# Decays, the copy of B and the order of products in a Mamba scan loop on one Trainium2 core

## What the kernel computes

```python
def step(h, inp):
    xh_t, B_t, C_t, dt_t, dA_t = inp
    h = dA_t[..., None, None] * h + (dt_t[..., None] * xh_t)[..., None] * B_t[:, None, None, :]
    y = jnp.einsum('bhpn,bn->bhp', h, C_t)
    return (h, y)
...
y = y + D[None, None, :, None] * xh
y = y * jax.nn.silu(z)
```

## Time and profile before

| what | value |
|---|---|
| median of 3 runs | 1082.24 us (1082.21 to 1082.91) |
| the profiled execution | 1084.32 us |
| its span in the profile | 1082.6 us |
| passes of the scan loop, DVE's first `dtx` to its last `H` | 741.62 to 825.32 us of the span, 83.7 us |
| busy in those 83.7 us | PE 64.6, DVE 63.7, POOL 48.3, ACT 24.0 us |

### The profile page before, as it was taken

How to read it: one execution, slowest core, us unless ns; L and a number is a source line. 1 busy time by engine, 2 the same in 40 slices (tenths; PEclk the granted TensorE clock), 3 DMA queues, 4 the chain that set the end, 5 groups by cost and what they waited for, 6 DMA issues and landing times. The chain is left out here.

```text
span 1082.6 us, 21285 instructions
## 1 busy us (share of the span) xinstructions
PE 949.9 (88%) x7613; PEld 563.9 (52%) x7613; DVE 801.6 (74%) x2128; ACT 681.7 (63%) x1049; POOL 500.9 (46%) x542
## 2 busy tenths in 40 slices
PE   3899999999999999969999999645878249999998
PEld 1323333333333333328878888323657238878886
DVE  7789999999989999755776554696675675775553
ACT  5226666666666665556888888583233138888886
POOL 4401201110121011116989999226562028989997
PEclk9869999999999999889999999887788669999999
DMA  4940322142222500025765675000000045667873
GB/s 104 248 154 17 102 78 58 40 132 51 58 80 84 100 3 3 2 68 154 192 186 148 196 194 133 20 1 0 0 0 1 3 104 161 198 171 168 213 193 97
DMA packets 80614, 105.93 MB, mean 98 GB/s; under 512 B 18252, under 2 KB 41602, under 8 KB 80514
## 3 DMA queue, kind: packets, MB, share of 16 engines
q1 hardware_dynamic: 78631, 102.43, 35.9%
q10 hardware_dynamic: 1883, 2.21, 0.7%
HBM read 95.84 MB, written 8.52 MB: 96 GB/s over the span
## 5 line engine op out<-in xcount | busy, mean ns | idle before, releaser
L801 POOL TENSOR_TENSOR f_act_low<-f_act,f_act_high 128x512 fp32r<-128x512 f32 x272 | 348.3, 1298 | 140.6 <-ACT f_act_high L777 132.8
L1710 DVE CUSTOM_DVE_ANT_0 at_rows<-at_rows,at_table_max 128x512 f32<-128x512 f32 x512 | 342.7, 717 | 38.6 <-PE at_rows L1488 29.0
L1657 ACT ACTIVATE at_prob<-at_cols 128x1024 f32<-128x1024 f32 x256 | 248.2, 1021 | 160.2 <-PE at_cols L1529 160.2
L816 DVE SCALAR_TENSOR_TENSOR f_gated<-f_hid,f_cw 128x512 f32<-128x512 f32 x256 | 176.0, 691 | 131.3 <-ACT f_act L782 91.4
L782 ACT ACTIVATE f_act<-f_gated 128x512 f32<-128x512 f32 x272 | 171.8, 632 | 85.7 <-DVE f_gated L816 68.1
L777 ACT CAST f_act_high<-f_act 128x512 fp32r<-128x512 f32 x272 | 164.7, 606 | 0.0
L1529 PE MATMUL at_cols<-at_table_cols,flip_sum 64*64 64x512 f16 x2048 | 138.4, 383 | 0.0
L1541 PE MATMUL at_pv<-at_prob,at_v_stack 128*32 128x512 f32 x1024 | 138.1, 612 | 0.4 <-ACT at_prob L1657 0.4
L1488 PE MATMUL at_rows<-at_k_stack,at_q_stack 48*64 48x512 bf16 x1024 | 117.0, 403 | 4.4 <-DVE at_maxima L1710 3.7
L748 PE MATMUL f_acc<-f_act_high,wd_high 128*128 128x512 f32 x272 | 107.8, 396 | 3.8 <-POOL f_act_low L801 3.8
L748 PE MATMUL f_acc<-f_act_low,wd_high 128*128 128x512 f32 x272 | 106.2, 391 | 0.0
(11 more groups left out here) (341 smaller groups left out, 1281.1 us busy)
## 6 DMA issues: line engine op xcount, KB each, us to landing
f_cw<-f_c_rows SPq DMA_DIRECT2D x256, 256.0 KB, 4.4
at_table_cols<-bias_rows SPq DMA_DIRECT2D x64, 124.0 KB, 4.3
at_table_max<-bias_rows SPq DMA_DIRECT2D x12, 480.0 KB, 4.6
at_q_stack<-q_parts SPq DMA_DIRECT2D x32, 96.0 KB, 2.5
at_k_stack<-k_parts SPq DMA_DIRECT2D x24, 96.0 KB, 3.4
at_raw_weights<-in_L_ffn_up_w_dram SPq DMA_DIRECT2D x8, 256.0 KB, 4.0
at_raw_weights<-in_L_ffn_down_w_dram SPq DMA_DIRECT2D x8, 256.0 KB, 5.1
at_table_max<-bias_rows ACTq DMA_DIRECT2D x4, 480.0 KB, 5.7
```

The lines of the kernel that those rows point to most:

```text
L801: nc.gpsimd.tensor_tensor(act_l[:, n % PART_SLOTS, :], act[:, n % ACT_SLOTS, :], act_h[:, n % PART_SLOTS, :].bitcast(F32), ALU.subtract).t ...
L816: ins = nc.vector.scalar_tensor_tensor(out=gated[:, n % GATE_SLOTS, :], in0=hid[:, n % HID_SLOTS, :], scalar=0.0, in1=cw[:, k % C_SLOTS, u ...
L1657: act(prob[:, S % 2, 2 * hp:2 * hp + 2, :], s2[:, hp, :, :], ACT.Exp).then_inc(exp_done, 1)
L1710: nc.vector.tensor_tensor_reduce(out=slot, in0=slot, in1=t_max[:, 2 * p.hp + j, c:c + BANK][:, ::-1], scale=1.0, scalar=-3.0e38, op0=ALU.a ...
```

## The change

`M` takes the decays from their PSUM bank, where ACT's exponential now leaves them; `E` is gone. The copy of B goes from DVE to ACT, behind the exponential of the same b and behind a wait on `dtx`. On DVE, `Ht` moves behind the `M` of its b, and both `dx` behind both `M`. On PE, both `inter` stand ahead of everything else that follows, and `dh` waits for `dx` as well, since `dx` reads the bank that the next pass's transposes overwrite.

```diff
-        E = sb("E", [P, 2, SH, P])
...
                         mm(ps[:, pb + 2, P:P + INNER], xch[:, b, 3, :], H[:, b, :, :].rearrange("p h c -> p (h c)"),
                            start=True, stop=True).then_inc(inter_done, 1)
-
+                    for b in range(SEQS):
+                        pb = 4 * b
                         pe.wait_ge(M_ready, n + (b + 1))
...
                         pe.wait_ge(btok_ready, n + (b + 1))
+                        pe.wait_ge(dx_ready, n + (b + 1))
...
-                        act(E[:, b, :, :], ps[:, 4 * b, :], ACT.Exp).then_inc(E_ready, 1)
+                        act(ps[:, 4 * b, :], ps[:, 4 * b, :], ACT.Exp).then_inc(E_ready, 1)
+                        a.wait_ge(dtx_ready, n + (b + 1))
+                        nc.scalar.copy(btok[:, b, :], ps[:, 4 * b + 1, INNER:INNER + P]).then_inc(btok_ready, 1)
...
-                        nc.vector.tensor_copy(btok[:, b, :], ps[:, pb + 1, INNER:INNER + P]).then_inc(btok_ready, 1)
-                        v.wait_ge(y3_ready, n + (b + 1))
-                        tt(dx[:, b, :, :], tok, dsk[:].unsqueeze(2).broadcast_to([P, SH, HEAD_COLS]), ALU.mult).then_inc(dx_ready, 1)
                         v.wait_ge(gt_done, n + (b + 1))
                         tt(Gm[:, b, :], ps[:, pb + 2, 0:P], m.upto[:], ALU.mult).then_inc(gm_ready, 1)
+                    for b in range(SEQS):
+                        t = bass.ds(i + b * SEQ_CHUNKS, 1)
+                        v.wait_ge(E_ready, n + (b + 1))
+                        v.wait_ge(gm_ready, n + (b + 1))
+                        tt(M[:, b, :, :], ps[:, 4 * b, :].rearrange("p (h j) -> p h j", h=SH), Gm[:, b, :].unsqueeze(1).broadcast_to([P, SH, P]),
+                           ALU.mult).then_inc(M_ready, 1)
                         tt(Ht[:, b, :, :], H[:, b, :, :],
...
                     for b in range(SEQS):
-                        v.wait_ge(E_ready, n + (b + 1))
-                        v.wait_ge(gm_ready, n + (b + 1))
-                        tt(M[:, b, :, :], E[:, b, :, :], Gm[:, b, :].unsqueeze(1).broadcast_to([P, SH, P]),
-                           ALU.mult).then_inc(M_ready, 1)
+                        tok = ps[:, 4 * b + 1, 0:INNER].rearrange("p (h c) -> p h c", h=SH)
+                        v.wait_ge(y3_ready, n + (b + 1))
+                        v.wait_ge(btok_ready, n + (b + 1))
+                        tt(dx[:, b, :, :], tok, dsk[:].unsqueeze(2).broadcast_to([P, SH, HEAD_COLS]), ALU.mult).then_inc(dx_ready, 1)
```

## The result

| | before | after |
|---|---|---|
| median | 1083.03 us (6 runs, 1082.21 to 1085.4) | 1073.89 us (6 runs, 1070.41 to 1076.57) |
| profiled execution, its span | 1084.32, 1082.6 us | 1073.45, 1071.7 us |
| scan loop, first `dtx` to last `H` | 83.70 us | 67.70 us |

The ratio is 0.9924 (95% interval 0.9907 to 0.9942), a gain of 9.1 us. The sign was right; 1073.89 lies far outside 1054 to 1064.5.

The account below looks back on a forecast made before the run. DVE and PE were taken to wait on each other in turn, with `M` held by POOL's `R`. The loop falls from 83.42 to 58.52 us, taking 1084.3 to 1059.4; less 2.1 to the median, 1057.3, range 1054 to 1064.5.

Parts of the forecast that it names:

- the price: `M` on DVE in the scan, one input now in PSUM: no longer held, 0.84 us less in each of seven passes.
- The edits costed at nothing: Exponential into PSUM at 0.60 us, `btok` on ACT, `inter` of b = 1 first: none was expected to lengthen a pass.
- The walk: Hand timeline of a new middle scan pass, timed from DVE's `dtx` of b = 0: 7.1 us, taken as 7.2.
- longest cycle: DVE from `dtx` of b = 1 to `dx`, then PE's `dh`, `intra`, `dh`, `tok`, `gt`, `seg`: 7.07 us a pass.
- DVE's own: Second cycle of the walked pass: DVE by itself, waiting only 0.16 for `tok`, 6.95 us.
- the 58.52 forecast: Whole scan loop after the change: first pass 8.67, six middle passes of 7.2, last pass 6.65 us.
- The step that failed: Start of the walked pass: DVE reaches `Ht` at 1.84 us, POOL begins `wxx` at 1.57 and `R` at 2.14.
- 1.7: Walk's start: the pass before has begun its last `dh` on PE 1.7 us before the `dtx` of b = 0.
- Both `Ht` meet an `R`: Rival, chance 0.16: POOL's `R` gets ahead and holds both `Ht`, `dx` at 4.63; pass 8.1, program 1062.7 us.
- The second rival: Chance 0.08: PE at 1.2 GHz in some passes, each then 10.8 us; two such passes give 1064.5 us.
- slower than before: Rival, chance 0.02: late `dx` widens PE's gap to 1.8 us, clock drops every pass; pass 11.8, program 1084.9 us.

Follow-up runs that it names:

- e4: The kernel before with only the exponential left in its PSUM bank and `M` reading it there; 1072.45 us, ratio 0.9899 to before.
- e1: The changed kernel with the decay factor of `Ht` read from spare PSUM columns; 1061.47 us, ratio 0.978 to before.
- e9: The changed kernel with the factor of `Ht` in PSUM and `dx` right behind `dtx`; 1057.11 us, ratio 0.9776 to before.
- e3: The changed kernel with the `intra` matmuls of b = 0 run twice over, same output; 1072.96 us, ratio 0.9896 to before.
- before_again: The kernel before, unchanged, traced a second time; one execution 1083.34 us, scan loop 79.98 us.
- again: The changed kernel, unchanged, run once more; 1073.51 us, ratio 0.9902 to before.
- e2: The changed kernel with each `dx` right behind its `dtx` again, ACT's copy of B behind it; 1065.78 us, ratio 0.9855 to before.
- e5: The changed kernel with `E` back in SBUF, the new order kept; 1081.8 us, ratio 0.9987 to before.

## Why the prediction was wrong

**Right: what bounded before, and the price.** `M` lost 0.84 us a pass and was never held; e4 shows that this, with the 1.6 us of clock that came with it, was the whole gain. `Ht` stayed exposed, as said. The edits costed at nothing (exponential, `btok` on ACT, `inter`) cost nothing: no wait of after names them. `dx` behind `M` wasn't free: e1 and e9 differ by 0.55 a pass. The walk had that price in its longest cycle.

**Right: the cycles, once `Ht` is free.** e1 has passes of 6.94 to 6.97 where the walk's longest cycle gave 7.07 and DVE's own 6.95. Its whole loop of 58.48 us beside the 58.52 forecast is luck in part: its first pass took 9.78, not 8.67 (its mean clock was 0.76), and its last 6.94 (6.91 up to the last `y3`, where the forecast ends), not 6.65, which the shorter middle ones made up.

**The step that failed: "`dtx` 0, `Gm` 0.34, `dtx` 0.70 ... `Ht` 1.84. POOL has begun `wxx` at 1.57".** In the long pass of after the second `dtx` is at 1.12 and `Ht` at 2.25, while `R` is at 2.17 against 2.14 walked. So POOL was placed well and DVE 0.4 us early. The walk let the next `dtx` of b = 0 follow the last `H` by 0.71, a distance from a row that itself shows DVE waiting (0.29 at 762.20). Where nothing is waited for, that distance is 0.45 (767.90 to 768.35 in e1). And the first `dtx` of the long pass comes 1.38 behind the last `dh` (751.88 to 753.26), not 1.7; with PE's 1.84 from that `dh` to the `tok` of b = 1, and 0.66 until DVE reads it instead of 0.54, the second `dtx` falls at 1.12. The same 1.38 was there to be read in before: `dh` of b = 1 from 749.94 on the earlier trace rows, `dtx` at 751.32. The margin by which `Ht` beat `R` in the walk was 0.3 us (1.84 to 2.14), less than the 0.42 by which the second `dtx` came later.

**So a rival was the case.** "Both `Ht` meet an `R`" was given 0.16 and a pass of 8.1, and was said to come seldom, since POOL's `wxx` would fall back to 1.56. It does fall back (1.60 in the long pass of after), and `R` is ahead all the same, since it was DVE that came later. When the first `R` ends, both engines start level and meet again at the second. e3 shows its price at the full clock, 8.5, because the second `Ht` is held in full too, so that `dx` is at 5.2 and not at 4.63. The second rival (clock, 0.08) came in on top, behind gaps of 1.93 us. Only the rival "slower than before" (0.02) let the late `dx` drop the clock, in every pass; it happened in every second one, which gave passes of 8.97, 8.32, 9.28, 8.05, 9.53 and 7.79 (51.9 us for 43.2 forecast).

**Where 16.6 us went.** From 1057.3 to 1073.89: the loop 9.2 (67.70 for 58.52); the scan's start 3.1 (744.73 for 741.62); behind the loop 2.0 (812.43 to 1071.7 is 259.3 us, before 257.3), less 0.3 for before's loop, which was summed as 83.42; and 2.5 from setting the profiled execution 2.1 over the median, while after's was 0.4 under. The start isn't the change's: before_again begins at 744.45. With it went a lower PE clock early in the attention. Stretches of 20 us, before first and then before again:

```profile
40.00:60.00 20.00, 16.58 (x84) 6.16 (x82) 19.39 (x61) 3.24 (x5) 6.64 (x16) 0.76 0.85 238
```

```profile
40.00:60.00 20.00, 19.50 (x80) 8.14 (x76) 17.94 (x54) 3.58 (x6) 5.33 (x11) 0.50 0.75 202
```

All 14 traces fall in two groups, whatever the kernel: with a clock of 0.71 to 0.79 in that stretch the scan begins at 739.1 to 741.8 (six traces), with 0.50 to 0.52 at 743.1 to 745.3 (eight). What decides between the two wasn't tried.

Part of the 2.0 behind the loop is the output projection, which ran at a lower clock: 0.82 from 812.43 to 831.00 in after, 0.89 from 825.32 to 841.00 in before. From its first matmul to its last it takes 12.6 us in after and again, 11.5 in both traces of before and in e2, and 11.7 to 12.8 in the other variants; no run isolates the cause. Even e1, whose loop is the forecast one, has 1061.47: some 4 of the miss were never the loop's.

## What to carry to other kernels

A DVE instruction with two SBUF inputs beside POOL's reads is a race for every pass. Where a hand walk leaves it a margin of some tenths of a us, price both outcomes and what the late one does to PE; better, take it out of the race (loops here shorter by 9.2 us with one input in PSUM, 13.3 with the work on another engine, 6.7 with POOL's order changed). Take an engine's own distances from passes in which it waits for nothing, and trace the kernel twice before making a sum against one execution. When one hold is removed, look for the next instruction of the same kind before reordering around it. And price a new wait by a run with and without it: here moving `dx` behind `M` cost 0.55 us a pass even with nothing held.

## What the runs showed of the hardware

- POOL and DVE held each other until the running instruction was through, where both read all their inputs from SBUF. An `Ht` 0.08 us behind `R` is held 0.83 us; an `Ht` or `M` that is waiting gets in between two POOL instructions, which makes the second `R` 1.22 (behind `Ht`) or 1.49 (behind an `M` with both inputs in SBUF, e5) us long instead of 1.04. The Trainium skill (page "SBUF — State Buffer", section "Who interferes with whom") says that a VectorE instruction with two SBUF inputs contends with a GpSimd one that reads SBUF, and one with at most one SBUF input doesn't. The traces agree on both: 1.24 for an `Ht` behind `R` in after, and in e1, with one input in PSUM, `Ht` lies inside `R` at 0.41.
- PE's granted clock stayed at 1.00 of 2.4 GHz through a gap of 1.43 to 1.82 us in each middle pass of e4, and fell in or behind passes with one of 1.93 (after) or 2.65 (e5). The length of the gap alone doesn't decide it: in before again it stayed at 1.00 through a pass with a gap of 2.67, and fell in the passes around it with gaps of the same length.
- An ACT exponential in place in PSUM took 0.58 us for 512 columns, 0.02 less than into SBUF.
